# A recurrence on one core: the output products of a block in three runs of eight instead of six runs of four

## The reference

```python
def step(h, inputs):
    ad, bd, xt, ct = inputs
    h = jnp.clip(h * ad[:, :, None] + bd[:, :, None] * xt[:, None, :], -10.0, 10.0)
    yt = jnp.einsum('bd,bdh->bh', ct, h)
    return (h, yt)
_, ys = jax.lax.scan(step, h0, (...))
y = ys.transpose(1, 0, 2) + D * xn
return y * jax.nn.silu(gate) @ W_out.T
```

## Time and profile before

| | us |
|---|---|
| median of 3 runs without a profile (4454.99 to 4455.63) | 4455.23 |
| the profiled execution, its own time | 4464.28 |
| span of that execution in the trace | 4462.5 |
| TensorE busy in the span (87%) | 3878.9 |
| VectorE busy in the span (65%) | 2910.5 |
| GpSimd busy in the span (41%) | 1827.7 |
| ScalarE busy in the span (30%) | 1319.1 |

### The profile page before, as it was taken

How to read it: one execution, slowest core, us unless ns; L and a number is a source line. 1 busy time by engine, 2 the same in 40 slices (tenths; PEclk the granted TensorE clock), 3 DMA queues, 4 the chain that set the end, 5 groups by cost and what they waited for, 6 DMA issues and landing times. The chain is left out here.

```text
span 4462.5 us, 67544 instructions
## 1 busy us (share of the span) xinstructions
PE 3878.9 (87%) x23976; PEld 2361.3 (53%) x23976; DVE 2910.5 (65%) x3006; ACT 1319.1 (30%) x1935; POOL 1827.7 (41%) x1464
## 2 busy tenths in 40 slices
PE   7999629999997599999758999996999907999999
PEld 5776403343332477777536777775766602433443
DVE  3666448999995556656356655643555537999996
ACT  3545301111113233333233333322444411111111
POOL 2555535555552123332312333322354434555555
PEclk9999758999998799999879999998999957999999
DMA  3556446555552122221221222113455535665553
GB/s 108 222 220 229 188 150 187 187 181 179 182 184 99 52 65 72 72 72 60 89 75 43 72 77 79 62 62 111 172 217 217 214 137 179 188 188 185 183 177 118
DMA packets 270300, 619.76 MB, mean 139 GB/s; under 512 B 34144, under 2 KB 36704, under 8 KB 270080
## 3 DMA queue, kind: packets, MB, share of 16 engines
q1 hardware_dynamic: 261408, 612.61, 41.5%
q10 hardware_dynamic: 8672, 4.14, 0.3%
HBM read 380.46 MB, written 236.19 MB: 138 GB/s over the span
## 5 line engine op out<-in xcount | busy, mean ns | idle before, releaser
L1083 DVE CUSTOM_DVE_ANT_0 l3r_g<-l3r_g,l3r_pv,l3r_cf 128x1024 f32<-128x1024 f32 x512 | 674.1, 1339 | 78.9 <-PE l3r_pv L945 53.4
L1083 DVE CUSTOM_DVE_ANT_0 l0r_g<-l0r_g,l0r_pv,l0r_cf 128x1024 f32<-128x1024 f32 x512 | 674.1, 1339 | 77.9 <-PE l0r_pv L945 44.4
L945 PE MATMUL l3r_pv<-l3r_x,l3r_wv 32*128 32x512 f32 x1024 | 260.7, 507 | 27.5 <-POOL l3r_wv L870 19.9
L957 PE MATMUL l3r_py<-l3r_g,l3r_cd 128*32 128x512 f32 x2048 | 280.2, 620 | 3.7 <-POOL l3r_cd L883 3.7
L945 PE MATMUL l0r_pv<-l0r_x,l0r_wv 32*128 32x512 f32 x1024 | 261.0, 509 | 25.5 <-POOL l0r_wv L870 19.1
L957 PE MATMUL l0r_py<-l0r_g,l0r_cd 128*32 128x512 f32 x2048 | 280.8, 621 | 1.8 <-POOL l0r_cd L883 1.8
L945 PEld LDWEIGHTS l3r_pv<-l3r_x,l3r_wv 32*128 32x128 f32 x1024 | 96.7, 186 | 328.0 <-issue 225.1
L945 PEld LDWEIGHTS l0r_pv<-l0r_x,l0r_wv 32*128 32x128 f32 x1024 | 96.9, 187 | 325.9 <-issue 223.8
L1683 DVE RECIPROCAL l1h_rec<-l1h_ps_o 128x256 f32<-128x256 f32 x64 | 112.3, 1755 | 120.3 <-PE l1h_ps_o L1486 120.2
L1683 DVE RECIPROCAL l2h_rec<-l2h_ps_o 128x256 f32<-128x256 f32 x64 | 112.3, 1755 | 119.9 <-PE l2h_ps_o L1486 119.8
L514 DVE SCALAR_TENSOR_TENSOR l3a_pacc<-l3a_pad,l3a_wconv,l3a_pacc 128x512 f32<-128x512 f32 x192 | 144.9, 754 | 33.9 <-ACT l3a_pacc L393 29.4
(11 more groups left out here) (390 smaller groups left out, 9844.8 us busy)
## 6 DMA issues: line engine op xcount, KB each, us to landing
xhl_s<-l0a_xo SPq DMA_DIRECT2D x128, 512.0 KB, 4.6
l0r_x<-xhl_s SPq DMA_DIRECT2D x128, 512.0 KB, 11.8
xhl_s<-l3a_xo SPq DMA_DIRECT2D x128, 512.0 KB, 4.6
l3r_x<-xhl_s SPq DMA_DIRECT2D x128, 512.0 KB, 11.9
gate_s<-l0a_gate SPq DMA_DIRECT2D x64, 256.0 KB, 2.4
dx_s<-l0a_dx SPq DMA_DIRECT2D x32, 512.0 KB, 5.0
l0r_crow<-feed_s SPq DMA_DIRECT2D x64, 256.0 KB
l0r_dx<-dx_s SPq DMA_DIRECT2D x32, 512.0 KB, 13.3
```

Source lines behind the costliest of these rows:

```text
L945: last = pe.matmul(pv[j % 2][:, h * HALF:(h + 1) * HALF], wv[r, q, 2 * t + j % 2, :], x[r, q, t, j % 2, :], start=True, stop=True)
L957: last = pe.matmul(py[j * JW:(j + 1) * JW, h * HALF:(h + 1) * HALF], cd[:, q, t, j, :], g[:, t, j, h * HALF:(h + 1) * HALF], start=t == 0, ...
L1083: dve._custom_dve(bass.dve_ops.TENSOR_ADD_SAT, out=g[:, t, j, :], in0=g[:, (t - 1) % TS, j, :], in1=pv[j % 2][:, :], s0=cf[:, q, t, 0, j:j ...
```

## The change

The table `MIX` shrinks from six places to three, and each place holds `RUN` = 8 products instead of 4. The places (0, 2), (1, 2) and (2, 2) stay empty: there the spread of j = 3 follows that of j = 2 with nothing between. The wait for the second half of `zl` moves from slot 3 to slot 1, which is the same place (2, 0). The instructions and their number are the same.

```diff
-        MIX = ((0, 2), (1, 0), (1, 2), (2, 0), (2, 2), (3, 0))
+        MIX = ((1, 0), (2, 0), (3, 0))
+        RUN = 3 * KI // len(MIX)
@@ def mix(k, slot)
-                if slot == 3:
+                if slot == 1:
                     pe.wait_ge(z_lo, 2 * k + 2)
-                for m in range(4 * slot, 4 * slot + 4):
+                for m in range(RUN * slot, RUN * (slot + 1)):
@@ def between(k, t, j, first, q)
-                elif not first:
+                elif not first and (t, j) in MIX:
                     mix(k - 2, MIX.index((t, j)))
```

## The result

The changed kernel takes 4467.19 us, median of ten runs, beside 4455.11 for the kernel before in ten runs. The ratio is 1.0024 with a 95% interval of 1.0015 to 1.0034: slower by 12 us (7 to 15). That is inside the range, and slower, as forecast.

The account below looks back on a forecast made before the run. TensorE's instruction stream was taken as the bound. Boundary +0.28 and two pairs at +0.06 made +0.40 us a block, +11.6 a layer; less 1.35, twice, +20.5 on 4455.2, stated as 4475 us, range 4457 to 4482.

Parts of the forecast that it names:

- What bounds the kernel: Steady blocks before the change: TensorE's own instruction stream sets the pace at 22.76 us a block, VectorE waiting a little each period.
- First, the edges: Entering and leaving a run of products on TensorE costs 0.22 us; three runs fewer save 0.66 us a block.
- Second, the pair of periods: Two periods around an empty place: waits for VectorE's updates make them 6.02 us against 5.96, +0.06, twice a block.
- the slower hand-over: A step's first spread starts 1.48 us after the update it waits for, not 1.39; the forecast with it had 55%.
- rival 2: A first spread's extra 0.09 us is hidden while the read-out runs: +6.4 us a layer, 4465 us in all; 28%.
- Third, the boundary: From a block's last eight products to the next block's first eight: 11.11 us against 10.83, +0.28, with spread (0,3) waiting.
- B: Spread that is second of a step, right behind a run of eight products; its start is time 0 in the prediction's timeline.
- The block: Steady block on TensorE: +0.40 us, giving 23.15 us; +0.22 without the later start of a step's first spread.
- Rival 1: Waits at empty places do not show, TensorE's own sum decides: 22.1 us a block, 41 us saved, 4414 us; 6%.
- Fourth, the end of the layer: Ahead of the last read-out stands one run of eight (2.04 us) instead of three of four (3.39): end 1.35 us earlier.
- The clock: TensorE's granted clock stays 1.00; a rival had it fall through waits, 4503 us if in one block of ten; 5%.

## Why the prediction was right in direction and too high

By its own steps:

- *What bounds the kernel* held. The kernel with half updates keeps 22.75: TensorE's list alone set the pace.
- *First, the edges* held as far as it went: eight products and their spread take 2.47 to 2.48 us (1005.33 to 1007.81), as the prediction had it. It left out that two spreads side by side also get 0.20 cheaper; the wait hides that, so the sum did not suffer.
- *Second, the pair of periods* is where the prediction failed, and the failed step is the choice of the slower hand-over, 1.48 for the first spread of a step. It is 1.40 in the loop's code, where 26 of 32 blocks run. The pair takes 5.89 to 5.93, the prediction's own number without it, not 6.02. The term was worth 0.18 of the 0.40 a block, 10 us in the sum, and it was given 55% against 28% although the row behind it stood in a block of other code. The reason given against rival 2, that nothing is behind the wait to hide it, was beside the point: there was nothing to hide. Where the code is written out the forecast's +0.40 is right: blocks 3 and 30 are 0.37 to 0.44 longer than before in each recurrence. Rival 2 had the size right for the loop, but not its reason, that the read-out ahead hides the extra time: written out, the same read-out stands ahead and the 0.09 is there.
- *Third, the boundary* held to 0.01: 11.10 for 11.11, and spread (0,3) at 7.21 after B (1007.81 to 1015.02). Four runs of six, which cover this one place, take the loss away. That the boundary costs 0.27 while each pair gains some 0.05 is the whole +0.17.
- *The block*: 22.92 where rival 2 said 22.95 and the forecast 23.15. The prediction's own terms give rival 2 22.76 + 0.22 = 22.98, and not 22.95; the gap to 22.92 is hundredths in the two pairs, and 22.76 for the 22.75 of before. Rival 1's list of 22.1 was too long: it is 21.50 without waits.
- *Fourth, the end of the layer.* The first and the last update of each recurrence, in the kernel before and in the changed one (one group of the tile each):

```profile
L1083 DVE CUSTOM_DVE_ANT_0 l0r_g<-l0r_g,l0r_pv,l0r_cf x512: 1327/1340/1344, 638.1 to 1378.0; 128x1024 f32<-128x1024 f32 x171
...
L1083 DVE CUSTOM_DVE_ANT_0 l3r_g<-l3r_g,l3r_pv,l3r_cf x512: 1330/1340/1344, 3691.3 to 4431.3; 128x1024 f32<-128x1024 f32 x171
```

```profile
L1084 DVE CUSTOM_DVE_ANT_0 l0r_g<-l0r_g,l0r_pv,l0r_cf x512: 1329/1336/1343, 634.1 to 1378.3; 128x1024 f32<-128x1024 f32 x171
...
L1084 DVE CUSTOM_DVE_ANT_0 l3r_g<-l3r_g,l3r_pv,l3r_cf x512: 1329/1336/1345, 3690.9 to 4436.6; 128x1024 f32<-128x1024 f32 x171
```

The second recurrence grew from 740.0 to 745.7 us, and from its last update to the end of the span it fell from 31.2 to 28.6: 2.6 shorter, where 1.35 was foreseen. Here the last two read-outs stand together and take 1.86 (4441.63 to 4443.48), as one row of sixteen matmuls shows:

```profile
4441.63 1.92 PE L958 MATMUL l3r_py<-l3r_g,l3r_cd 128*32 128x512 f32 x16
...
4443.48 0.50 PE L980 MATMUL l3r_po<-l3r_wol,l3r_zh 128*128 128x512 f32 x1
...
4443.62 1.03 ACT L1027 ACTIVATE l3r_y<-l3r_py 128x1024 f32<-128x1024 f32 x1 [4.52 <-PE l3r_py L958]
```

ScalarE's copy of y starts 7.0 after the last update (4443.62 - 4436.6), and 8.7 before (4439.98 - 4431.3): 1.7 of the 2.6. That is the 1.35 of the prediction and 2 x 0.14, since the two read-outs ahead of the run stand together too. The rest lies behind the copy, and is the clock's and not the change's:

```profile
4440.00:4462.50 22.50, 12.50 (x44) 9.10 (x44) 0.00 (x0) 4.66 (x7) 9.74 (x6) 0.82 0.10 35
4443.60:4465.20 21.60, 12.20 (x48) 9.06 (x48) 0.00 (x0) 4.67 (x7) 9.75 (x6) 0.86 0.11 36
```

From the copy of y to the end the granted clock was 0.82 before and 0.86 after: 18% and 14% of these stretches lost, 4.0 and 3.0 us. In the first layer it was the other way: from the copy of y to the last copy to `mixed` it took 17.0 us before and 18.0 after, in the second 17.4 and 16.5.

- *The clock* stayed at 1.00 in both stretches, as held likely, with TensorE busy 97% of the time. It did not in the order with two runs of twelve.

The sum as the traces give it, from update to update: the first recurrence +4.3 (739.9 to 744.2), the second +5.7, from the last update of the first to the first of the second -0.7 (2313.3 to 2312.6), the end -2.6: together +6.7. (Ahead of the first recurrence, in phases that the change doesn't touch, the trace after is 4.0 shorter, 634.1 for 638.1; hence the 2.7 between the spans.)

Not all of that is the change's. In the first three blocks of a recurrence the granted clock moves, and they took 81.5 and 81.7 us before, 80.2 and 81.8 after. From the first update of block 3 to the last of the recurrence the clock was 1.00, and the two recurrences grew from 658.3 to 664.1 and from 658.3 to 663.9. With the copy of y 1.6 earlier in each, these parts come to +8.0 us. That lies within the 7 to 15 measured. The 4 us up to the median of +12 have no place in the traces; the ten runs of the changed kernel alone spread over 9 us, and this remainder was not settled.

So the direction and the boundary were understood, and the forecast's size was not. The measured time lies inside the range because the range was drawn wide enough to take in rival 2. Rival 2's own +10 comes near to the +12 partly by luck: it gave the end 1.35 a layer for 1.6, took the loop's block 0.05 too high, and did not know of the written-out blocks.

## What to carry to other kernels

Filler between two double-buffered engines is priced by the place where it stands: a piece that runs while the other engine has both halves full costs little, and the same piece behind a single refill makes that engine wait, which a light stretch later did not win back here. So fewer, longer pieces save edges, but whatever in a piece is longer than the other engine's work in hand comes back as a wait. Of the orders tried, the one with refills in pairs ahead of the pieces was the fastest, though it also had the shortest list. Take the price of a hand-over from rows of the code form that runs most often, a loop's body before written-out first blocks. Look at the granted clock whenever a change makes waits longer.

## What the runs showed of the hardware

- Two adjacent pairs of 32-row matmuls take 0.66 us, and 0.86 with something of another shape between; two adjacent read-outs 1.86 instead of 2.00; entering and leaving a run of 128x128 products cost 0.22. The Trainium skill, "TensorEngine Tiling (Array Packing)", Tiling Modes, says that changing the tiling mode drains TensorE. These prices agree with it in kind, and so does the direction of the 1.25 us a block on TensorE's own list; the page gives no price, and no word on what the waits take back.
- A first spread of a step, held by VectorE's update, started 1.49 us after that update's start in written-out code and 1.40 in the loop's code, both at granted clock 1.00.
- In the order with two runs of twelve, where TensorE stood idle for up to 0.76 us at a time, the granted clock fell in eleven blocks (0.93 over the block from 1051.6 to 1077.2 us). In the changed kernel, with idle times of at most 0.5 us, it was 1.00 through all blocks from the fourth on.
- VectorE's updates follow one another at 1.25 us though each is recorded as 1.34 long, and in the loop a spread that waits starts 1.39 to 1.40 after the update's start, some 0.06 after its recorded end.
